# A differential attention and feed-forward block: projections and scores in split 16-bit halves, with scales worked out on chip

## The chip, the cores and the metric

The kernel runs on one core of one Trainium2 chip. The metric is the device time in microseconds of one execution. Engines are called PE (TensorE), DVE (VectorE), ACT (ScalarE), POOL (GpSimd) and SP (SyncE), as in the profile.

## The reference, cut to what matters

The input `x` is 2048 tokens of 256 numbers (float32). In short:

```python
def attn(x):
    qkv = x @ Wqkv.T + bqkv            # 16 query heads, 8 key heads of 128; 4 value heads of 256
    # 8 output heads; head h has two maps, each with its own query and key head
    p1 = softmax(causal(q[h, 0] @ k[h // 2, 0].T / sqrt(128)))
    p2 = softmax(causal(q[h, 1] @ k[h // 2, 1].T / sqrt(128)))
    o = (p1 - lam * p2) @ v[h // 2]    # lam from four vectors
    o = o / rms(o) * subln_w * (1 - LAMBDA_INIT)
    return concat(o) @ out_w.T + out_b

def ffn(x):                            # fwht: normalised Walsh-Hadamard transform
    x = fwht(x * SU_ug) / 64
    x = silu(x @ W_gate.T * s_gate) * (x @ W_up.T * s_up)
    return fwht(x * SU_dp) / 64 @ W_down.T * s_down

x = x + layernorm(attn(layernorm(x)))
x = x + layernorm(ffn(layernorm(x)))
```

All inputs and the output are float32.

## The kernel before, in words

**Split products.** A product of float32 matrices is made of three matmuls: each factor is split into a high half (a rounded copy, written by ACT) and a low half (what is left, written by DVE as source minus high half), and high x high, high x low and low x high are summed in PSUM. For the input, the weights of queries, keys and values, and the queries and keys themselves the halves are `float32r` (tiles `xT_hi`/`xT_lo`, `wq_*`, `wkv_*`, `q_*`, `k_*`). The probabilities, the values, the attention output and its weights are already split in 16-bit halves (`p16`, `v16`, `o16`, `wo16`), with a scale that keeps them in the range of the type: for the values `v_scale`, from a bound that is worked out on chip from the sum of squares of the weights (steps CV and CS).

**Tiling.** Tokens are cut in 16 tiles of 128. The 4 groups (one value head each, two key heads `m`, four query heads) are worked through in turn. A group has 16 duos (`d`, 64 in all), a duo two query tiles (`o`), a long and a short one, together 17 key blocks of 128, in 5 chunks `j` of up to 512 keys. For each duo and map `m` a step S makes the scores of a chunk: three matmuls (lines 1038, 1041, 1044) into one of four score banks. DVE then takes the chunk's maximum (line 1441), or, for the last chunk of a tile, adds the causal mask and takes the maximum in one instruction (line 1436; line 1431 where the tile has one chunk only, directly with the sign turned). If the tile has more chunks than one, line 1445 reduces the maxima to `negmx`, after a wait for the instruction before it. ACT's step E (line 1211) takes the exponential out of the score bank, with `negmx` as bias and the sum of the row as a second result. The query weights hold the factor 1/sqrt(128) already (`scale=SCALE` in WQ), so the exponential's scale is the constant 1.0 or -1.0. DVE then makes `ratio` and `gain` (SUMS, INV, GAIN: lines 1718, 1723, 1733, 1736). The second map's exponentials are scaled by `ratio` on ACT (line 1226) or POOL (line 1782), added to the first's on POOL (line 1749), split in halves on ACT (line 1233) and DVE (line 1452), transposed by DMA, and multiplied with the values in step PV (lines 1065 to 1067). The output of a tile is normed (lines 1241, 1708, 1756, 1249, 1482), transposed by DMA and multiplied with the output weights in step OP (line 1118).

**Projections.** QP makes a query head for 256 tokens (six matmuls, line 1137; halves by lines 1267 and 1494), K a key head for 512 tokens (line 1082; 1275 and 1502), V the values of 256 tokens (line 1100; 1515, 1280, 1790). They are six matmuls per 256 or 512 columns (V: twelve). The keys of the next group are written over those of this one, so that K of map 0 stands among the last scores of a group, and K of map 1 among the first of the next.

**Order of the work.** `plan()` goes through the whole work once, ahead of time, with a cost and a rank for each step of each engine (`add(...)` in `spawn`), and what it depends on (`needs`). PE takes the first step of its streams that may start; another engine takes the ready one of the lowest rank. The result is a fixed order of instructions for each engine; at run time each engine goes through its list in order and waits on semaphores. The start is written out by hand in `FIRST_STEPS`: LN and NX norm the input, X transposes it (line 1020; 1291 and 1547), IDLE are transposes of no use that keep PE busy, and WK, WQ, WV split the weights (ACT lines 1304, 1297, 1307; DVE lines 1567, 1557, 1571). CQ and CV (DVE lines 1462 and 1468, PE line 1050) and CS (DVE line 1476, POOL lines 1814 to 1822) work out the scale of the values. SP's queue loads at the start, in this order: two pieces of `x`, the key and value weights of the first group, a third piece of `x`, `col` (columns of biases and scales), the lambda vectors, `bv` (the value biases, broadcast), `out_b_row`. ACT's queue loads two pieces of `x`, the query weights of the first group and a last piece of `x`.

**The feed-forward part.** Its weights are folded with the transform on the chip in the last group: HAD and FB on POOL, FH (lines 1334, 1616), the matmul F (line 1147) and its eviction by ACT (line 1352) and DVE (line 1624) into places that `wug` names, among them the last quarter of `k_hi` and `k_lo` (F 0 and 1), `wq_hi` and `wq_lo` (F 4 and 5). F 0 and 1 therefore wait for the last score that reads a late key (`last_late_key`), F from 4 for the last query projection. Z transposes the normed rows into the columns of `xT_*` that queries no longer need (line 1154; 1367, 1640), and waits for a late query projection. Evictions of F and Z have rank 2. A step that holds one of the four work banks of PSUM (`turn_bank` 0 and 1, `sum_bank`, `proj_bank`) keeps it until its eviction has run, and PE's next step for that bank waits. G and U (line 1172) are the gate and up products, DN (lines 1189, 1191) the down product.

## Time and profile before

| | us |
|---|---|
| median of 3 runs | 1286.78 |
| lowest and highest | 1283.31, 1291.37 |
| the profiled execution | 1285.75 |
| its span in the trace | 1283.5 |

The span runs from the first to the last instruction of the profiled execution; some 2 us lie around it. A row of a group gives engine, line, operation, output<-inputs, shapes and count, then the busy time in us and the mean of one in ns, and after the second bar the idle time of the engine just before these instructions and what ended it. PEld are PE's weight loads, which overlap its matmuls. Matmuls overlap each other too, so their pace is read from start to start in a timeline, not from their length. A clock of 1.00 in a window is the full 2.4 GHz.

### The profile page before, as it was taken

To read this page: it belongs to the slowest core of one execution; us is meant where nothing else is said; L and a number is where in the kernel's file an instruction comes from. 1 tells how busy PE (TensorE), PEld (TensorE's weight loads), DVE (VectorE), ACT (ScalarE), POOL (GpSimd) and SP (SyncE) were. 2 spreads that over 40 slices of the span, in tenths; PEclk is the share of its full clock that TensorE was granted. 3 is DMA by queue.
4 is the path that set the end of the run, shared out by engine and by line. 5 is a ranking of instruction groups with operands and counts; after the bars stand their busy time and mean duration, and the time that the engine had idled before them with its cause. 6 is when DMAs were issued, how large, how long until landed. Compare 5 with 4: busy or idle time off the path is not lost.

```text
span 1283.5 us, 26516 instructions
## 1 busy us (share of the span) xinstructions
PE 1210.5 (94%) x8102; PEld 1018.7 (79%) x8102; DVE 1066.1 (83%) x2876; ACT 995.4 (78%) x2599; POOL 700.8 (55%) x797
## 2 busy tenths in 40 slices
PE   8899999999999999999999999999988797898998
PEld 7787887877888878888878788788876685786887
DVE  6889999888789998989799989888889899637545
ACT  5788888889688888978789889887877788745341
POOL 3464645454655655536565655445588574556532
PEclk9899999999999999999999999999998899999999
DMA  3145545564265554532555455445543453720001
GB/s 128 57 76 105 88 85 89 102 101 71 50 127 90 99 91 89 103 70 55 126 97 95 85 94 102 74 75 114 100 85 76 93 90 69 143 46 1 29 17 37
DMA packets 368154, 106.62 MB, mean 83 GB/s; under 512 B 359312, under 2 KB 365712, under 8 KB 367504
## 3 DMA queue, kind: packets, MB, share of 16 engines
q1 hardware_dynamic: 366672, 103.37, 42.6%
q8 instruction: 67, 1.10, 0.4%
q10 hardware_dynamic: 1344, 1.57, 0.3%
q14 instruction: 71, 0.58, 0.1%
HBM read 14.71 MB, written 2.10 MB: 13 GB/s over the span
## 4 chain that ended last, share of the span: by engine, by line
PE 47%; DVE 29%; issue 8%; ACT 8%; POOL 4%; DMA 4%; SPq 1%; ACTq 0%; DVEq 0%; POOLq 0%
DVE p L1452 7%; PE score_bank L1172 7%; DVE mx L1441 6%; PE score_bank L1038 5%; PE score_bank L1044 4%; PE score_bank L1041 4%; ACT e_all L1211 4%; DVE score_bank L1436 4%; PE turn_bank L1065 2%; POOL e_all L1749 2%; PE turn_bank L1066 2%; PE turn_bank L1067 2%; DMA p16T<-p 2%; PE proj_bank L1065 2%; PE proj_bank L1067 2%
## 5 line engine op out<-in xcount | busy, mean ns | idle before, releaser
L1749 POOL TENSOR_TENSOR e_all<-e_all 128x512 f32<-128x512 f32 (+3 forms) x320 | 372.9, 1179 | 141.9 <-ACT e_all L1226 131.6
L1211 ACT ACTIVATE e_all<-score_bank,negmx 128x512 f32<-128x512 f32 (+2 forms) x640 | 394.1, 625 | 60.8 <-DVE negmx L1445 46.3
L1038 PE MATMUL score_bank<-k_hi,q_hi 128*128 128x512 f32 (+2 forms) x640 | 257.1, 402 | 32.9 <-ACT e_all L1211 16.9
L1452 DVE SCALAR_TENSOR_TENSOR p<-e_all,gain,p 128x512 f16<-128x512 f32 (+3 forms) x320 | 266.2, 846 | 9.3 <-ACT p L1233 8.9
L1441 DVE TENSOR_REDUCE mx<-score_bank 128x1 f32<-128x512 f32 (+1 forms) x384 | 242.5, 636 | 18.3 <-PE score_bank L1044 17.4
L1041 PE MATMUL score_bank<-k_lo,q_hi 128*128 128x512 f32 (+2 forms) x640 | 233.0, 364 | 0.4 <-DVE k_lo L1502 0.4
L1044 PE MATMUL score_bank<-k_hi,q_lo 128*128 128x512 f32 (+2 forms) x640 | 233.1, 364 | 0.0
L1233 ACT ACTIVATE p<-e_all,gain 128x512 f16<-128x512 f32 (+3 forms) x320 | 203.9, 665 | 13.0 <-POOL e_all L1749 12.6
L1038 PEld LDWEIGHTS score_bank<-k_hi,q_hi 128*128 128x128 f32 x640 | 121.7, 190 | 75.6 <-ACT e_all L1211 33.6
L1782 POOL TENSOR_SCALAR e_all<-e_all,ratio 128x512 f32<-128x512 f32 (+3 forms) x123 | 89.6, 728 | 156.8 <-DVE ratio L1733 155.9
L1756 POOL TENSOR_TENSOR few<-few,half_neg 128x1 f32<-128x1 f32 x128 | 78.5, 614 | 142.0 <-DVE few L1708 141.8
L1065 PE MATMUL turn_bank<-v,p16T 128*128 128x256 f16 x553 | 152.4, 276 | 3.7 <-DVE q_lo L1494 1.7
L1066 PE MATMUL turn_bank<-v,p16T 128*128 128x256 f16 x553 | 151.6, 274 | 0.0
L1067 PE MATMUL turn_bank<-v,p16T 128*128 128x256 f16 x553 | 151.5, 274 | 0.0
L1226 ACT ACTIVATE e_all<-e_all,ratio 128x512 f32<-128x512 f32 (+2 forms) x197 | 121.5, 660 | 16.5 <-DVE ratio L1733 16.3
L1044 PEld LDWEIGHTS score_bank<-k_hi,q_lo 128*128 128x128 f32 x640 | 121.5, 190 | 14.0
L1211 ACT ACTIVATION_READ_ACCUMULATOR e_all<-score_bank,negmx 128x1 f32 x640 | 131.9, 206 | 0.0
L1041 PEld LDWEIGHTS score_bank<-k_lo,q_hi 128*128 128x128 f32 x640 | 122.3, 191 | 7.0 <-DVE k_lo L1502 0.6
L1436 DVE CUSTOM_DVE_ANT_0 score_bank<-score_bank,mask 128x384 f32<-128x384 f32 (+2 forms) x192 | 110.7, 577 | 14.7 <-PE score_bank L1044 14.3
L1065 PE MATMUL proj_bank<-v,p16T 128*128 128x256 f16 x326 | 89.4, 274 | 0.0
L1067 PE MATMUL proj_bank<-v,p16T 128*128 128x256 f16 x326 | 89.0, 273 | 0.0
L1066 PE MATMUL proj_bank<-v,p16T 128*128 128x256 f16 x326 | 89.0, 273 | 0.0
(393 smaller groups left out, 2738.6 us busy)
## 6 DMA issues: line engine op xcount, KB each, us to landing
p16T<-p SPq DMA_TRANSPOSE x320, 3.1
w_raw<-in_w_qkv_dram SPq DMA_DIRECT2D x3, 1024.0 KB, 5.3
w_raw<-in_w_o_dram SPq DMA_DIRECT2D x4, 512.0 KB, 3.3
oT<-o SPq DMA_TRANSPOSE x128, 2.5
bv<-in_hidden_dram SPq DMA_DIRECT2D x8, 256.0 KB, 2.9
w_raw<-in_w_ug_dram SPq DMA_DIRECT2D x4, 512.0 KB, 4.3
out_dram<-e SPq DMA_DIRECT2D x16, 128.0 KB, 1.7
e<-in_w_d_dram SPq DMA_DIRECT2D x1, 1024.0 KB, 5.9
```

Of the source, the lines that this page charges most:

```text
L1038: pe.matmul(bank[:, 0:w], qh, kh, start=True, stop=False)
L1041: pe.matmul(bank[:, 0:w], qh, kl, start=False, stop=False)
L1044: pe.matmul(bank[:, 0:w], ql, kh, start=False, stop=True).then_inc(s_full, 1)
L1065: pe.matmul(bank[:, 0:HID], hi, v16[:, kt, 0, :], start=(kt == 0), stop=False)
L1066: pe.matmul(bank[:, 0:HID], hi, v16[:, kt, 1, :], start=False, stop=False)
L1067: mm = pe.matmul(bank[:, 0:HID], lo, v16[:, kt, 0, :], start=False, stop=(kt == i))
L1211: act.activation(e, S[k % NS][:, 0:w], ACT.Exp, bias=negmx[:, d % 2, m, s:s + 1], scale=-1.0 if alone else 1.0, accum_out=ssum[:, d % 4, s ...
L1233: act.activation(halves_of(q, w)[0], e1_of(q, w), ACT.Copy, scale=gain[:, d % 4, s:s + 1]).then_inc(p_hi, 1)
L1436: dve.tensor_tensor_reduce(out=S[k % NS][:, 0:w], in0=S[k % NS][:, 0:w], in1=mask[:, BANK - w:], scale=1.0, scalar=LOWEST, op0=ALU.add, op ...
L1441: dve.tensor_reduce(mx[:, d % 2, m, s, c:c + 1], S[k % NS][:, 0:w], X, ALU.max)\
L1452: dve.scalar_tensor_tensor(out=halves_of(q, w)[1], in0=e1_of(q, w), scalar=gain[:, d % 4, s:s + 1], in1=halves_of(q, w)[0], op0=ALU.mult, ...
L1749: pool.tensor_tensor(a, a, b, ALU.add).then_inc(p_pool, 1)
```

## The change

The input (`x16`, scaled by 8), the weights (`wq16`, `wkv16`), the queries (`q16`) and the keys (`k16`) become 16-bit halves. The scales of queries, keys and values come from bounds worked out on chip: CQ squares the query weights on ACT, CV the biases and the key and value weights on DVE, PE adds over the partitions with two matmuls, CS on DVE and POOL makes `w_scale` and `scale` and scales the biases `col` and `bv`, and a new step CU on DVE makes `unit`, 1/sqrt(128) over the product of the scales of queries and keys. The scores are then `1/unit` too large in PSUM; the exponential takes `unit` as its scale, the maxima are multiplied with it. WK, WQ and WV of a group wait for CS. Keys lie in two buffers, used in turn by the groups. Homes of feed-forward weights and rows move to where no score or query of the last group reads, and the waits of F and Z for them go. In `plan()` some costs are changed, and evictions of F and Z get better ranks.

```diff
 FIRST_STEPS = (
-    ("LN", 0), ("LN", 1), ("NX", 0), ("WK", 0), ("NX", 1), ("IDLE", 38), ("X", 0), ("X", 1), ("IDLE", 8),
-    ("X", 2), ("X", 3), ("IDLE", 8), ("WQ", 0), ("LN", 2), ("K", (0, 1, 0)), ("K", (0, 0, 0)),
+    ("LN", 0), ("LN", 1), ("NX", 0), ("NX", 1), ("CQ", 0), ("IDLE", 38), ("X", 0), ("X", 1), ("CV", 0), ("CS", 0),
+    ("IDLE", 8), ("X", 2), ("X", 3), ("WK", 0), ("WQ", 0), ("LN", 2), ("IDLE", 8), ("K", (0, 1, 0)), ("K", (0, 0, 0)),
...
-SCORE_US, VALUE_US = 0.00136, 0.00257
+SCORE_US, VALUE_US = 0.00129, 0.00257
...
-            add("S", "DVE", "S", what, (0.17 if last else 0.07) + 0.00104 * w + (0.15 if last and c else 0), [pe], 0)
+            unit = [] if d % DUOS else [("DVE", "CU", d // DUOS)]
+            add("S", "DVE", "S", what, (0.17 if last else 0.07) + 0.00104 * w + (0.25 if last and c else 0), [pe] + unit, 0)
...
-                    "WK": [("PE", "V", (g - 1, V_UNITS - 1))] if g else [], "WV": [("POOL", "CS", g)]}[kind]
+                    "WK": [("PE", "V", (g - 1, V_UNITS - 1))] if g else [], "WV": []}[kind] + [("POOL", "CS", g)]
...
         elif kind == "CQ":
-            add("Y", "DVE", "CV", what, 1.1, [], 1)
+            add("Y", "ACT", "CQ", what, 1.1, [], 1)
+            add("Y", "DVE", "CV", what, 2.4, [], 1)
         elif kind == "CS":
             add("Y", "DVE", kind, what, 0.2, [("PE", "CV", what)], 0)
-            add("Y", "POOL", kind, what, 1.6, [("DVE", kind, what)], 0)
+            add("Y", "POOL", kind, what, 2.8, [("DVE", kind, what)], 0)
+            add("Y", "DVE", "CU", what, 0.6, [("POOL", kind, what)], 0)
...
         elif kind == "Z":
-            add("O", "ACT", kind, what, 0.7, [pe], 2)
-            add("O", "DVE", kind, what, 0.72, [("ACT", kind, what)], 2)
+            add("O", "ACT", kind, what, 0.7, [pe], 0)
+            add("O", "DVE", kind, what, 0.72, [("ACT", kind, what)], 1)
...
         elif kind == "F":
-            add("O", "ACT", kind, what, 0.7, [pe], 2)
-            add("O", "DVE", kind, what, 0.75, [("ACT", kind, what)], 2)
+            add("O", "ACT", kind, what, 0.7, [pe], 0)
+            add("O", "DVE", kind, what, 0.75, [("ACT", kind, what)], 1)
...
         if kind == "F":
-            return [("DVE", "FH", what)] + ([("PE", "S", last_late_key)] if what < 2 else
-                                             [("PE", "QP", (ALL_DUOS // 2 - 1, 1, 1))] if what >= 4 else [])
+            return [("DVE", "FH", what)]
         if kind == "Z":
-            return [("ACT", "N", (what[0], 3, half)) for half in range(2)] + [("PE", "QP", (ALL_DUOS // 2 - 5, 1, 1))]
+            return [("ACT", "N", (what[0], 3, half)) for half in range(2)]
...
-        xT_hi = sb("xT_hi", [P, CT, SEQ], F32R)
-        xT_lo = sb("xT_lo", [P, CT, SEQ], F32R)
+        zT_at = sb.at()
+        zT = sb("zT", [P, FFN_CHUNKS, 2, CT, BANK], F32R)
+        x16 = placer(nc, zT_at + 16 * CT * BANK)("x16", [P, 2, CT, SEQ], F16)
...
+            k16 = placer(nc, sa.at())("k16", [P, 2, 2, 2, SEQ], F16)
             k_hi = sa("k_hi", [P, 2, SEQ], F32R)
             k_lo = sa("k_lo", [P, 2, SEQ], F32R)
...
-                        kh = k_hi[:, m, key:key + w]
-                        kl = k_lo[:, m, key:key + w]
+                        kh = k16[:, d // DUOS % 2, m, 0, key:key + w]
+                        kl = k16[:, d // DUOS % 2, m, 1, key:key + w]
...
-                                   scale=-1.0 if alone else 1.0, accum_out=ssum[:, d % 4, s, m, c:c + 1]).then_inc(s_act, 1)
+                                   scale=-1.0 if alone else unit[:, g], accum_out=ssum[:, d % 4, s, m, c:c + 1]).then_inc(s_act, 1)
...
                             dve.tensor_tensor_reduce(out=S[k % NS][:, 0:w], in0=S[k % NS][:, 0:w],
-                                                     in1=mask[:, BANK - w:], scale=-1.0, scalar=HIGHEST,
+                                                     in1=mask[:, BANK - w:], scale=neg_unit[:, g], scalar=HIGHEST,
...
                             dve.wait_ge(s_dve, k + 1)
-                            dve.tensor_reduce(negmx[:, d % 2, m, s:s + 1], mx[:, d % 2, m, s, 0:c + 1], X,
-                                              ALU.max, negate=True).then_inc(neg_ready, 1)
+                            dve.tensor_reduce(neg_raw[:, d % 2, m, s:s + 1], mx[:, d % 2, m, s, 0:c + 1], X,
+                                              ALU.max, negate=True).then_inc(raw_ready, 1)
+                            dve.wait_ge(raw_ready, neg_use[o, m] + 1)
+                            dve.tensor_tensor(negmx[:, d % 2, m, s:s + 1], neg_raw[:, d % 2, m, s:s + 1], unit[:, g],
+                                              ALU.mult).then_inc(neg_ready, 1)
...
                     elif kind == "CV":
                         if what == 0:
+                            dve.wait_ge(cols_landed, 16)
+                            dve.wait_ge(rows_landed, 32)
+                        else:
+                            dve.wait_ge(bound_full, what)
+                        at = K_COL + 2 * what
+                        for n, bias in ((0, col[:, 4 * what:4 * what + 4]), (1, col[:, at:at + 2]), (2, bv[:, what, :])):
+                            dve.tensor_tensor_reduce(out=squares_b[:, n, 0:bias.shape[-1]], in0=bias, in1=bias,
+                                                     scale=1.0 / P if n == 2 else 1.0, scalar=0.0, op0=ALU.mult,
+                                                     op1=ALU.add, accum_out=wb_sq[:, n:n + 1]).then_inc(sq_ready, 1)
+                        if what == 0:
                             dve.wait_ge(first_w_landed, 16)
...
+                        for n in (1, 2):
+                            part = w_raw[:, :, BANK + (n - 1) * HID:BANK + n * HID]
+                            dve.tensor_tensor_reduce(out=squares_w[:, n - 1, :, :], in0=part, in1=part, scale=float(HID),
+                                                     scalar=0.0, op0=ALU.mult, op1=ALU.add,
+                                                     accum_out=w_sq[:, n:n + 1]).then_inc(sq_ready, 1)
...
+                    elif kind == "CU":
+                        g = slice(what, what + 1)
+                        dve.wait_ge(scale_ready, 2 * what + 2)
+                        dve.tensor_tensor(both[:, 0:1], scale[:, what, 0:1], scale[:, what, 1:2], ALU.mult)\
+                           .then_inc(unit_step, 1)
+                        dve.wait_ge(unit_step, 2 * what + 1)
+                        dve.reciprocal(both[:, 1:2], both[:, 0:1]).then_inc(unit_step, 1)
+                        dve.wait_ge(unit_step, 2 * what + 2)
+                        dve.tensor_scalar(unit[:, g], both[:, 1:2], SCALE, None, ALU.mult).then_inc(unit_ready, 1)
+                        dve.tensor_scalar(neg_unit[:, g], both[:, 1:2], -SCALE, None, ALU.mult).then_inc(unit_ready, 1)
```

The 16-bit forms of the other instructions follow the same pattern: `x16`, `wq16`, `wkv16`, `q16` in the place of the float32r tiles, in QP, K, V and X. ACT's WQ, WK and WV read their scale per partition from `w_scale`.

## Rows read from the trace of the kernel before

**Rows 1.** The page, part 1: busy time, share of the span, instructions of each engine.
```profile
PE 1210.5 (94%) x8102; PEld 1018.7 (79%) x8102; DVE 1066.1 (83%) x2876; ACT 995.4 (78%) x2599; POOL 700.8 (55%) x797
```

**Rows 2.** Busy time by windows: length, engines' busy us (instructions), clock, DMA share, GB/s.
```profile
100.00:900.00 800.00, 776.81 (x5485) 656.72 (x5484) 709.93 (x1935) 682.72 (x1834) 434.61 (x475) 1.00 0.50 91
400.00:500.00 100.00, 97.64 (x687) 81.55 (x685) 92.88 (x260) 90.90 (x250) 59.03 (x65) 1.00 0.50 88
600.00:700.00 100.00, 97.64 (x725) 83.76 (x725) 85.18 (x237) 80.58 (x218) 54.84 (x59) 1.00 0.52 100
900.00:1130.00 230.00, 199.86 (x1361) 164.70 (x1360) 195.66 (x524) 179.79 (x476) 146.06 (x173) 0.95 0.50 94
1130.00:1283.00 153.00, 145.03 (x718) 119.79 (x716) 82.01 (x190) 62.08 (x116) 73.93 (x82) 0.99 0.07 21
```

**Rows 3.** Timeline of PE from 400 us: start us, length us, engine, line, operands.
```profile
399.84 0.27 PE L1065 MATMUL turn_bank<-v,p16T 128*128 128x256 f16 x1
...
400.71 0.27 PE L1067 MATMUL turn_bank<-v,p16T 128*128 128x256 f16 x1
...
401.18 0.40 PE L1038 MATMUL score_bank<-k_hi,q_hi 128*128 128x512 f32 x1
...
401.88 0.40 PE L1137 MATMUL sum_bank<-xT_hi,wq_hi 128*128 128x256 f32 x2
...
402.58 0.39 PE L1038 MATMUL score_bank<-k_hi,q_hi 128*128 128x512 f32 x1
```

**Rows 4.** Groups by line: weight loads, float32 and 16-bit; busy us, mean ns, idle before.
```profile
L1041 PEld LDWEIGHTS score_bank<-k_lo,q_hi 128*128 128x128 f32 x640 | 122.3, 191 | 7.0 <-DVE k_lo L1502 0.6
...
L1066 PEld LDWEIGHTS turn_bank<-v,p16T 128*128 128x128 f16 x553 | 54.6, 99 | 5.7
```

**Rows 5.** Groups by line and form on ACT: busy us, mean ns, idle us before.
```profile
L1211 ACT ACTIVATE e_all<-score_bank,negmx 128x512 f32<-128x512 f32 x320 | 217.9, 687 | 45.3 <-DVE negmx L1445 37.9 <-DMA p16T<-p 5.7 <-DVE negmx L1431 0.2
...
L1375 ACT ACTIVATE acc<-acc,n_shift,n_rs 128x256 f32<-128x256 f32 x16 | 8.5, 591 | 0.3 <-POOL n_shift L1874 0.3
...
L1226 ACT ACTIVATE e_all<-e_all,ratio 128x256 f32<-128x256 f32 x7 | 3.5, 503 | 0.3 <-DVE ratio L1733 0.2
...
L1291 ACT ACTIVATE xT_hi<-turn_bank 128x512 fp32r<-128x512 f32 x4 | 2.3, 596 | 1.6 <-PE turn_bank L1020 1.6
...
L1352 ACT ACTIVATE spare<-turn_bank,su_s 128x512 fp32r<-128x512 f32 x2 | 1.4, 688 | 0.2 <-PE turn_bank L1147 0.2
```

**Rows 6.** Timeline of DVE from 441.98 us.
```profile
441.98 0.14 DVE L1436 DVE_READ_ACCUMULATOR2_ANT mx<- 128x1 f32 x1
442.15 0.16 DVE L1445 TENSOR_REDUCE negmx<-mx 128x1 f32<-128x3 f32 x1
442.23 0.22 DVE L1733 SCALAR_TENSOR_TENSOR ratio<-s,inv,neg_lam 128x1 f32<-128x1 f32 x1
```

**Rows 7.** Groups by line on DVE: negmx, and two low halves.
```profile
L1494 DVE SCALAR_TENSOR_TENSOR q_lo<-turn_bank,bq,q_hi 128x256 fp32r<-128x256 f32 x65 | 30.8, 475 | 2.4 <-ACT q_hi L1267 2.2
...
L1482 DVE SCALAR_TENSOR_TENSOR o<-turn_bank,few,o 128x256 f16<-128x256 f32 x63 | 30.0, 477 | 10.0 <-ACT o L1249 9.9
...
L1445 DVE TENSOR_REDUCE negmx<-mx 128x1 f32<-128x2 f32 (+1 forms) x192 | 29.9, 156 | 6.6
```

**Rows 8.** Timeline of the start, all engines.
```profile
4.13 0.68 SPq L914 DMA_DIRECT2D bv<-in_rows_dram  x1
...
15.24 0.71 PE L1082 MATMUL turn_bank<-xT_hi,wkv_hi 128*128 128x512 f32 x2
...
28.28 0.68 DVE L1462 CUSTOM_DVE_ANT_1 squares<-w_raw 128x512 f32<-128x512 f32 x1
...
31.39 0.19 POOL L1817 TENSOR_SCALAR few<-few 128x1 f32<-128x1 f32 x1
```

**Rows 9.** DMA issues: queue, operation, count, KB each, us to landing.
```profile
bv<-in_rows_dram SPq DMA_DIRECT2D x1, 512.0 KB, 9.9
```

**Rows 10.** Waits of PE, 1000 to 1060 us: us in total, times, longest us.
```profile
PE turn_bank L1137 <- DVE spare L1624: 6.9, 1, 6.9
```

More of the change, by code:

```diff
@@ L429, in needs @@
         if kind == "CV":
-            return [("DVE", "CV", what)]
+            return [("DVE", "CV", what), ("ACT", "CQ", what)]
         if kind == "OV":
@@ L1290, in _ @@
                         act.wait_ge(t_full, t_use[kind, what] + 1)
[L1291 to L1293 removed]
+                        act.activation(x16[:, 0, ct, q * BANK:(q + 1) * BANK], bank_for(kind, what)[:, :], ACT.Copy,
+                                       scale=X_UNIT).then_inc(t_hi, 1)
+                    elif kind == "CQ":
@@ L1294, in _ @@
                         act.wait_ge(w_landed, 16 * (2 * what + 1))
                         if what > 0:
+                            act.wait_ge(bound_full, what)
+                            act.wait_ge(sq_ready, 5 * what)
+                        act.activation(squares[:, :, :], w_raw[:, :, 0:BANK], ACT.Square, scale=float(HID) ** 0.5,
+                                       accum_out=w_sq[:, 0:1]).then_inc(sqq_ready, 1)
+                    elif kind == "WQ":
+                        act.wait_ge(scale_ready, 2 * what + 2)
+                        if what > 0:
```

297 lines of the change are left out of this document (144 added, 153 removed), and 4 rows, old and new, of the table FIRST_STEPS.

## The prediction

> **What bounds the kernel now.** I read the page first: the reader is to see PE busy for 94% of the span, DVE for 83%, ACT for 78%, POOL for 55% [rows 1]. Overlapping matmuls make a busy PE say little, so I took the windows next [rows 2]. In 100 to 900 us DVE is busy 709.9 and ACT 682.7 of 800 us. This stretch is no uniform one: of its eight windows of 100 us, four look like 400 to 500 us (DVE 92.88, ACT 90.90) and four like 600 to 700 us (DVE 85.18, ACT 80.58). After 900 us PE loses its density (199.9 of 230), and from 1130 us the feed-forward part runs, which the change leaves in float32.
>
> Third, the timeline of PE gives the pace from start to start [rows 3]. Eight 16-bit matmuls of 256 columns lie between 399.84 and 400.71: 0.1088 us each. Three float32 ones of 512 columns take 401.18 to 401.88, 0.2333 each, and six of 256 columns take 401.88 to 402.58, 0.1167 each. In 100 to 900 us the groups by form count 3021 matmuls of the first kind, and float32 columns worth 1803 matmuls of 512 columns: 1803 x 0.2333 + 3021 x 0.1088 = 749 us, 94% of the stretch. In 400 to 500 us the same sum gives 93.8, in 600 to 700 us 95.0. So PE bounds the light windows alone, while in the heavy ones DVE and ACT stand one to three points behind it. That is what decides this change: it takes work from PE and gives work to the two next in line.
>
> **What PE saves.** Scores, queries, keys and values turn 16-bit. No row has a 16-bit matmul of 512 columns; two of 256 make 0.2175, so I take 0.0158 saved per 512 columns. Bounds: zero, and 0.0316 if the fixed part of a matmul were all that changed. Scores: 3 x 278,528 columns are 1632 such units, 25.8 us; queries (128 x 6 of 256 columns) and values (32 x 12 of 256) 576 units, 9.1 us; keys (32 x 6) 192 units, 3.0 us. Sum 38 us, of which 1803 x 0.0158 = 28.5 fall in 100 to 900 us. Weight loads shrink from 191 to 99 ns [rows 4]; that is hidden while PE streams and is worth 0.09 us only where PE had waited, so I count it within the bounds.
>
> **What ACT gains.** The exponential (L1211) had a scale written into the instruction and a bias read per partition; now 576 of its 640 instructions (all but the 64 of rows of one chunk) read both per partition. Rows on what one such operand costs: Copy of 512 columns out of PSUM 596 ns with none, 688 ns with one; 256 columns in SBUF 503 ns with one, 591 ns with two [rows 5]. So 0.09 us each, 576 x 0.09 = 52 us, 40 of them in 100 to 900 us, 5.0 per window. Bounds: zero and 0.09. No row has an exponential with both.
>
> The Trainium skill (ScalarE: Activation LUTs, section "What ACT_TABLE_LOAD costs") says that each such pointer operand adds about 93 ns. The rows agree with 92 and 88 ns; for the exponential with two, no row here shows it, and by the page the term would be 54 us. It is the rule that speaks most against this change.
>
> CQ adds one square over 1024 columns per group on ACT; from 596 ns for 512 columns I estimate 1.0 to 1.3 us, four times, 5 us spread out. WK and WV keep their length but for one operand.
>
> **What DVE gains.** Each of the 192 masked maxima with more chunks than one now ends in two small instructions, the negated maximum and its product with `unit`, and the second waits for the first. The row for such a wait is the accumulator read at 441.98, followed by L1445 at 442.15: 0.17 us; with no dependence the next starts 0.08 us later, at 442.23 [rows 6]. I take 0.17 (the new one waits the same way): 192 [rows 7] x 0.17 = 33 us, 25 of them in 100 to 900 us, 3.1 per window. Bounds 0.08 and 0.25, so 15 to 48 us. Queued behind it stand the next maximum and the low halves; the exponential waits for it, and PE's next score for the bank.
>
> The Trainium skill (VectorE: DVE Perf Modes, section "The DRAIN you can't avoid") holds that a semaphore after every instruction costs nothing extra. The row here shows 0.09 us more with the wait than without, for instructions this small; by the page this term would be 15 us and the total some 5 us lower.
>
> The 64 single-chunk maxima (L1431) read their scale per partition: between 0 and 0.09 us by ACT's rows, 3 us. The low halves cost the same in either type: 475 ns to float32r, 477 ns to 16 bits [rows 7]; zero, hidden or not. CV grows by three sums of squares and CU adds four small instructions: about 1.6 us per group, 6 us. POOL's CS grows by some 1.2 us per group; POOL's 45% of idle covers it, except at the start.
>
> **The main stretch.** A heavy window after: PE 93.8 - 3.4 = 90.4, DVE 92.9 + 3.1 = 96.0, ACT 90.9 + 5.0 = 95.9. Before, DVE had 7.1 and ACT 9.1 us of idle there. With all of it kept the window takes 103 to 105, with half kept 99.5 to 100.5; I take 101.5, since in-order engines that wait for each other keep some. A light one: PE 95.0 - 3.4 = 91.6, DVE 88.3, ACT 85.6: PE still ends last, with its former 5 us of gaps 96.6; I take 97. Four of each: 794, so 6 us are won of 800. Ends: all of PE's 28.5 won; 20 lost (105 four times).
>
> **The start.** All projections now wait for the scales. DVE's CV begins with the biases, and `bv` is issued at 4.13 and lands 9.9 later, at 14.0 [rows 8, 9]; nothing behind CV on DVE (the low halves of X) runs before. Before, the same chain from squares (28.28) to the scale on POOL (31.39 + 0.19) took 3.3 us [rows 8]; with four more sums, some 1.5 us, it ends near 18.8. ACT's WK (0.75) brings the first key to 19.6, where it started at 15.24 [rows 8]. 4.3 later, less a little since CV, CS no longer break in at 28 us: +4. Ends 0 and +8, the upper one if PE's clock falls in the pause. The cover is gone here: nothing else can run.
>
> **The last group.** Keys of group 3 lie in the second buffer, and z in columns of its own, so F and Z need no late score or query any more, and their evictions get the first rank on ACT. That removes the wait of a query projection for the bank that an F held, 6.9 us [rows 10], and perhaps 5 us of smaller ones and of lowered clock (0.95 in 900 to 1130 us [rows 2]). DVE is late next: its 195.7 us of 230 grow by 7. Net -5; ends -20 and +7. The two key buffers move no key projection: the list of steps keeps their places. They are costed at nothing, for PE's order already kept them apart. The feed-forward part: 0, within 2.
>
> **Sum.** Against the profiled execution (1285.75 us for a span of 1283.5): 1285.75 + 4 - 6 - 5 = 1278.75, say 1279. That execution lies 1.0 under the median of the runs shown (1286.78), well inside their spread, so I add nothing.
>
> **Rivals.**
> *PE stays the only bound.* For it: PE's sum is the highest in every window, and the gaps of DVE are mostly waits for others. Against it: DVE and ACT at 96% of a heavy window. Then 38 us go, and of the last group 7: 1285.75 + 4 - 38 - 7 = 1245; half way to it is likelier, so 1250.
> *ACT takes PE's place.* The exponential's second operand, in heavy windows: ACT keeps the 9.1 us it waits for maxima and lands at 105, while `plan` still gives E its old cost and moves no scaling to POOL. It decides once ACT stays above some 91% busy, its share there now. 4 x 5 = 20, start 4, the last group nothing: 1310. Against it: PE's and DVE's earlier scores shorten those waits.
> *The last group clears wholly* (-20, the rest as forecast): 1264.
> *The 16-bit matmuls stream no faster at 512 columns,* so the change doesn't do what it says: the heavy windows slow, the light ones stay, 1296.
>
> **How the numbers follow.** Chances: the forecast 0.42 (its own range 1266 to 1292), PE alone 0.25, ACT 0.22, the last group 0.07, no faster stream 0.04. Range 1252 to 1304: it cuts the outer half of the two large rivals. About 1% (1274 and 1300) is what a measurement of this kernel can tell from no change. Faster by over 1%: 0.25 + 0.07 + 0.07 of the forecast's own 0.42 = 0.39. Slower: 0.19 of ACT's 0.22 and 0.01 of the last = 0.20. Between: 0.41.
>
> **What would show it.** L1211's successor at about 0.09 us more for each form; negated maximum and product 0.17 us apart, 192 times; score matmuls of 512 columns near 0.2175 us; the first key near 19.6 us; in heavy windows DVE and ACT at 95% or more and PE's sum near 90; no wait of PE for a held F bank. Wrong it would be if the exponential kept 687 ns, if heavy windows held no more than 93% of DVE (then PE alone bounds), or if the first key came by 16 us.

## The result and the profile after

| | us |
|---|---|
| before, median of 4 runs | 1285.43 |
| after, median of 4 runs (1333.32 to 1337.74) | 1334.20 |
| ratio, 95% interval | 1.0377 [1.0336, 1.0417] |
| after, the profiled execution and its span | 1334.5, 1332.7 |
| forecast (range) | 1279 (1252 to 1304) |

The change costs 49 us where the forecast had it win 7. The page of the kernel after, part 1 (busy time by engine) and the first line of part 4 (the chain that ended last, by engine):

```profile
PE 1184.8 (89%) x8110; PEld 831.2 (62%) x8110; DVE 1133.7 (85%) x3107; ACT 1040.1 (78%) x2596; POOL 700.3 (53%) x820
...
DVE 48%; PE 21%; issue 11%; ACT 10%; DMA 6%; POOL 2%; SPq 1%; ACTq 0%; DVEq 0%; POOLq 0%
```

Against [rows 1], PE lost 26 us of busy time and five points of its share. DVE gained 68 us, ACT 45. Nearly half of the chain now runs over DVE, where the page of before has 47% of it on PE and 29% on DVE:

```profile
PE 47%; DVE 29%; issue 8%; ACT 8%; POOL 4%; DMA 4%; SPq 1%; ACTq 0%; DVEq 0%; POOLq 0%
```
The windows, columns as in [rows 2]:

```profile
100.00:900.00 800.00, 722.42 (x5185) 493.62 (x5186) 722.98 (x2006) 681.73 (x1749) 414.87 (x472) 0.99 0.48 85
400.00:500.00 100.00, 88.48 (x631) 59.57 (x628) 94.53 (x280) 86.32 (x222) 55.92 (x64) 0.98 0.50 88
600.00:700.00 100.00, 91.67 (x701) 66.33 (x700) 89.70 (x255) 81.32 (x211) 55.97 (x58) 1.00 0.48 89
900.00:1130.00 230.00, 199.02 (x1442) 137.85 (x1439) 211.84 (x568) 191.18 (x481) 143.37 (x173) 0.99 0.48 89
```

In 800 us PE gets through 5185 matmuls where it got through 5485, though each is cheaper. DVE is busier in every window, ACT not: ACT's share fell in 400 to 500 us from 90.9 to 86.3, so it waits. For whom, the waits say (us in total, times, longest):

```profile
ACT e_all L1225 <- DVE negmx L1465: 83.2, 113, 2.5
...
PE score_bank L1050 <- ACT e_all L1225: 41.3, 68, 2.3
...
PE score_bank L1050 <- issue: 28.5, 50, 2.2
```

The exponential waits 83 us for the scaled maximum; before, it waited 46 for the maximum. Groups by line and form on ACT and DVE:

```profile
L1225 ACT ACTIVATE e_all<-score_bank,negmx,few 128x512 f32<-128x512 f32 x304 | 234.4, 776 | 79.0 <-DVE negmx L1465 72.1 <-DMA p16T<-p 5.3 <-DVE p L1472 1.1
L1225 ACT ACTIVATE e_all<-score_bank,negmx,few 128x384 f32<-128x384 f32 x256 | 170.8, 672 | 15.9 <-DVE negmx L1465 11.1 <-DMA p16T<-p 4.4
...
L1465 DVE TENSOR_TENSOR negmx<-few 128x1 f32<-128x1 f32 x192 | 74.0, 385 | 6.6
```

The first answers to the 687 ns of [rows 5]: 776, the 0.09 us of the forecast. The last is the surprise: a product of one number per partition, at 385 ns on average, 74 us in all. Its line by itself (shortest, median and longest in ns) shows that most are short and some very long:

```profile
L1465 DVE TENSOR_TENSOR negmx<-few x192: 159/161/1282, 33.2 to 1162.4; 128x1 f32<-128x1 f32 x192
```

Two timelines of the same moment, DVE's and then POOL's, show what a long one is:

```profile
1124.64 0.16 DVE L1462 TENSOR_REDUCE few<-mx 128x1 f32<-128x3 f32 x1
1124.83 1.26 DVE L1465 TENSOR_TENSOR negmx<-few 128x1 f32<-128x1 f32 x1
1126.01 0.68 DVE L1458 TENSOR_REDUCE mx<-score_bank 128x1 f32<-128x512 f32 x1
```

```profile
1124.02 0.70 POOL L1804 TENSOR_SCALAR e_all<-e_all,ratio 128x512 f32<-128x512 f32 x1
1124.81 1.26 POOL L1771 TENSOR_TENSOR e_all<-e_all 128x512 f32<-128x512 f32 x1
1126.06 0.59 POOL L1804 TENSOR_SCALAR e_all<-e_all,ratio 128x384 f32<-128x384 f32 x1
```

POOL's sum of the two maps starts at 1124.81 and ends at 1126.07; DVE's product starts 0.02 us behind it and ends at 1126.09. Over the whole trace, of the 81 products that start while POOL is idle none takes more than 0.25 us, of the 111 that start while POOL is at work 82 do. The reduce before it (L1462), with one tensor as input, takes 154 to 160 ns whatever POOL does.

Not every instruction of POOL holds the product up. Nine products start inside one of POOL's small powers (x to the -0.5, on one to four columns: L1778, L1904) with 0.16 us or more of it left, and all take 159 to 161 ns. This power runs from 140.61 to 141.16, and the product in it is short:

```profile
140.61 0.55 POOL L1778 TENSOR_TENSOR few<-few,half_neg 128x1 f32<-128x1 f32 x1
```

```profile
140.72 0.16 DVE L1465 TENSOR_TENSOR negmx<-few 128x1 f32<-128x1 f32 x1
```

The start, in the timeline (DVE's squares of the biases, PE's first matmul of the bounds, of a key and of a score):

```profile
15.07 0.16 DVE L1483 CUSTOM_DVE_ANT_0 squares_b<-col 128x4 f32<-128x4 f32 x1 [4.24 <-DMA out_b_row<-in_rows_dram]
```

```profile
17.04 0.59 PE L1063 MATMUL proj_bank<-few,ones 128*128 128x3 f32 x2 [6.63 <-DVE few L1492]
...
22.91 0.59 PE L1095 MATMUL turn_bank<-x,wkv 128*128 128x512 f16 x2
...
29.23 0.38 PE L1050 MATMUL score_bank<-k,q 128*128 128x512 f16 x1
```

The first key comes 7.7 us later than in [rows 8]. At the other end stand PE's last score matmuls, of before and of after:

```profile
1110.38 0.33 PE L1044 MATMUL score_bank<-k_hi,q_lo 128*128 128x384 f32 x1
```

```profile
1161.10 0.33 PE L1056 MATMUL score_bank<-k,q 128*128 128x384 f16 x1
```

They lie 51 us apart, so the whole loss stands ahead of the feed-forward part. Each of the four groups has 160 chunks of scores. Cut at every 160th of the chunks' last matmuls, the four stretches take 277.3, 282.3, 282.3 and 289.5 us, before 268.5, 264.8, 265.7 and 289.5: 8 us are lost before the first score, 43 in the first three stretches and none in the last.

### The profile page after: what moved, and what is told of

Its sections match the earlier page's. It is cut to its first block, busy times and chain, and to the rows that moved or that the text cites. A ratio compares the mean times of both kernels' runs of the same rounds, so it can differ in the third digit from the quotient of the medians.

```text
span 1332.7 us, 26815 instructions
## 1 busy us (share of the span) xinstructions
PE 1184.8 (89%) x8110; PEld 831.2 (62%) x8110; DVE 1133.7 (85%) x3107; ACT 1040.1 (78%) x2596; POOL 700.3 (53%) x820
## 4 chain that ended last, share of the span: by engine, by line
DVE 48%; PE 21%; issue 11%; ACT 10%; DMA 6%; POOL 2%; SPq 1%; ACTq 0%; DVEq 0%; POOLq 0%
DVE p L1472 11%; DVE mx L1458 9%; ACT e_all L1225 6%; PE score_bank L1185 6%; DVE score_bank L1453 6%; DMA p16T<-p 4%; DVE negmx L1465 3%; DVE q L1526 2%; DVE acc L1565 2%; DVE o L1514 2%; DVE few L1462 2%; PE score_bank L1050 1%; DMA oT<-o 1%; DVE ratio L1755 1%; PE score_bank L1056 1%
## 5 line engine op out<-in xcount | busy, mean ns | idle before, releaser
L1225 ACT ACTIVATE e_all<-score_bank,negmx,few 128x512 f32<-128x512 f32 (+2 forms) x576 | 413.3, 724 | 95.0 <-DVE negmx L1465 83.2
L1771 POOL TENSOR_TENSOR e_all<-e_all 128x512 f32<-128x512 f32 (+3 forms) x320 | 364.7, 1153 | 94.7 <-ACT e_all L1240 83.5
L1050 PE MATMUL score_bank<-k,q 128*128 128x512 f16 (+2 forms) x640 | 227.0, 355 | 74.6 <-ACT e_all L1225 41.3
L1472 DVE SCALAR_TENSOR_TENSOR p<-e_all,gain,p 128x512 f16<-128x512 f32 (+3 forms) x320 | 257.4, 822 | 5.2 <-ACT p L1247 4.9
L1053 PE MATMUL score_bank<-k,q 128*128 128x512 f16 (+2 forms) x640 | 225.9, 353 | 0.3 <-DVE k L1533 0.3
L1056 PE MATMUL score_bank<-k,q 128*128 128x512 f16 (+2 forms) x640 | 225.8, 353 | 0.0
L1804 POOL TENSOR_SCALAR e_all<-e_all,ratio 128x512 f32<-128x512 f32 (+2 forms) x134 | 92.8, 693 | 214.8 <-DVE ratio L1755 214.2
L1050 PEld LDWEIGHTS score_bank<-k,q 128*128 128x128 f16 x640 | 62.9, 98 | 176.0 <-ACT e_all L1225 82.1
L1778 POOL TENSOR_TENSOR few<-few,half_neg 128x1 f32<-128x1 f32 x128 | 78.8, 617 | 170.4 <-DVE few L1730 170.4
L1240 ACT ACTIVATE e_all<-e_all,ratio 128x384 f32<-128x384 f32 (+2 forms) x186 | 115.0, 659 | 8.9 <-DVE ratio L1755 8.2
L1225 ACT ACTIVATION_READ_ACCUMULATOR e_all<-score_bank,negmx,few 128x1 f32 x576 | 116.7, 203 | 0.0
L1056 PEld LDWEIGHTS score_bank<-k,q 128*128 128x128 f16 x640 | 63.3, 99 | 58.1 <-issue 3.5
L1078 PE MATMUL sum_bank<-v,p16T 128*128 128x256 f16 x306 | 84.6, 276 | 12.3 <-DMA p16T<-p 8.7
L1080 PE MATMUL sum_bank<-v,p16T 128*128 128x256 f16 x306 | 84.8, 277 | 0.0
L1079 PE MATMUL sum_bank<-v,p16T 128*128 128x256 f16 x306 | 84.6, 277 | 0.0
L1465 DVE TENSOR_TENSOR negmx<-few 128x1 f32<-128x1 f32 x192 | 74.0, 385 | 6.6
```

The costliest lines, as they stand in the source:

```text
L1050: pe.matmul(bank[:, 0:w], qh, kh, start=True, stop=False)
L1053: pe.matmul(bank[:, 0:w], qh, kl, start=False, stop=False)
L1056: pe.matmul(bank[:, 0:w], ql, kh, start=False, stop=True).then_inc(s_full, 1)
L1078: pe.matmul(bank[:, 0:HID], hi, v16[:, kt, 0, :], start=(kt == 0), stop=False)
L1079: pe.matmul(bank[:, 0:HID], hi, v16[:, kt, 1, :], start=False, stop=False)
L1080: mm = pe.matmul(bank[:, 0:HID], lo, v16[:, kt, 0, :], start=False, stop=(kt == i))
```

## The experiments

Three theories. **A:** DVE has become the bound, and the product is dear because its instruction, with two tensors in SBUF as inputs, is held up while POOL works. **B:** ScalarE's scale pointer costs it. **C:** the order that `plan` writes out. Ratios are to the kernel before, run on the same chip. Its median there was 1283.5 to 1286.5 us, so a difference of 2 or 3 us between kernels of different batches says nothing.

### The product, one edit at a time on the kernel after

**e1_ts** exchanges the instruction:

```diff
-dve.tensor_tensor(negmx[...], neg_raw[...], unit[:, g], ALU.mult)
+dve.tensor_scalar(negmx[...], neg_raw[...], unit[:, g], None, ALU.mult)
```

> The kernel after, with one instruction exchanged: the product that scales the row maximum (192 times a 128x1 result) reads its second factor as a per-partition pointer (tensor_scalar) and no longer as a second tensor (tensor_tensor). Theory A (VectorE has become the bound, and the product is dear because an instruction with two tensors in SBUF is held up while GpSimd works: mean 385 ns, shortest 159, longest 1282): the product falls to about 160 to 200 ns, VectorE gives back 35 to 43 us of busy time, and the time falls by at least 20 us, to 1295 to 1314. Theory B (ScalarE's second pointer on the exponential, 0.09 us each, some 52 us, is what costs): the product may get shorter, the time stays within 1% of 1334. Theory C (the new order of the engines' queues costs): the same, within 1%.

1305.2 us, ratio 1.0158 [1.0117, 1.0200]: 29 us back for one operand read another way, within theory A's range. Its line:

```profile
L1465 DVE TENSOR_SCALAR negmx<-few x192: 211/214/216, 33.2 to 1134.2; 128x1 f32<-128x1 f32 x192
```

It is slower than the shortest tensor_tensor (159) and never slower than 216. Two of A's figures are just missed: the product was to fall to 200 ns or less, and DVE was to give back at least 35 us; it gives back 33.6 (1100.1 for 1133.7). The exponential's wait for it falls from 83.2 to 53.8.

**e2_nomul** takes the product out, and leaves out the subtraction of the row maximum (the exponential still waits for the reduce):

```diff
-dve.tensor_reduce(neg_raw[...], mx[..., 0:c + 1], X, ALU.max, negate=True).then_inc(raw_ready, 1)
-dve.wait_ge(raw_ready, neg_use[o, m] + 1)
-dve.tensor_tensor(negmx[...], neg_raw[...], unit[:, g], ALU.mult).then_inc(neg_ready, 1)
+dve.tensor_reduce(negmx[...], mx[..., 0:c + 1], X, ALU.max, negate=True).then_inc(neg_ready, 1)
-act.activation(e, S[...], ACT.Exp, bias=negmx[...], ...)
+act.activation(e, S[...], ACT.Exp, bias=few[:, 116:117], ...)   # zeros
```

> The kernel after without the product: the row maximum is written by the reduce alone, and the exponential reads a column of zeros as its bias, so the subtraction of the row maximum is left out; its wait on the reduce stays, as does the scale pointer. Theory A: 74 us of VectorE's busy time go; the time falls by 40 us or more, to 1270 to 1295. Theory B: ScalarE is unchanged and the time stays at 1320 or above. Theory C: 1320 or above.

1282.2 us, 0.9976 [0.9957, 0.9994]. The product costs 52 us in all: 29 the stall, 23 the steady form of the instruction and its wait. DVE's busy time falls by 63.0 us (1070.7 for 1133.7), not by the 74 expected. A group's busy time adds up its instructions one by one, and the page counts the time in which they overlap once. Besides, DVE's low halves of the probabilities (`p`, also with two tensors in SBUF) take 262.5 us here for 257.4, which fits a part of the stall moving to another instruction.

**e3_imm** has an immediate for the scale pointer, and leaves out the right scale of the scores:

```diff
-scale=-1.0 if alone else unit[:, g], accum_out=...
+scale=-1.0 if alone else 1e-6, accum_out=...
```

> The kernel after with an immediate (1e-6) as the exponential's scale in place of the pointer (the right scale of the scores is left out); the product stays. ScalarE gives back about 0.09 us on 560 exponentials, 50 us. Theory B: the time falls by 30 us or more, to 1305 or lower. Theory A: the score bank comes free 0.09 us sooner at best, VectorE stays the bound: 1320 to 1334.

1318.5 us, 1.0267 [1.0227, 1.0306]: 16 us back, and one exponential of 512 columns takes 687 ns again. It falls between the theories: 1.5 us under what A allowed, 13 above what B wanted. ACT's busy time fell by 48 us, so a third of it shows.

**e4_both** has both edits of e2_nomul and e3_imm, and leaves out the same.

> Neither the product nor the pointer: bias a column of zeros, scale an immediate (row maximum and scale of the scores are left out). What is left of the change is 16-bit operands, the two key buffers, the bounds at the start and the order. If A or B or both hold, the time falls to 1245 to 1270, which is what the 40 us that TensorE saved allow with TensorE as the only bound. Theory C (order): it stays above 1285.

1268.5 us, 0.9877 [0.9839, 0.9915]: 14 us under e2_nomul. A and B add up: 52 and 14 to 16.

### The same two costs on the kernel before

**b_tt** and **b_ts** add the product to the kernel before, by a column of ones, in either form; **b_ptr** adds the pointer (`scale=-1.0 if alone else few[:, 54:55]`).

```diff
+dve.wait_ge(raw_ready, neg_use[o, m] + 1)
+dve.tensor_tensor(negmx[...], neg_raw[...], few[:, 54:55], ALU.mult)        # b_tt
+dve.tensor_scalar(negmx[...], neg_raw[...], few[:, 54:55], None, ALU.mult)  # b_ts
```

> The kernel before with the product alone: the row maximum is multiplied by a column of ones in a tensor_tensor of two SBUF operands, 192 times. Theory A (the instruction is held by GpSimd, whatever the rest): its mean is 300 to 450 ns with instances above 1 us, VectorE gets 60 to 85 us more, and the time rises by 15 to 50 us to 1300 to 1335. If only the kernel after's order makes the product dear, its mean is under 200 ns and the time stays within 1%.

> The kernel before with the product (by one) as a tensor_scalar, that is b_tt with its second factor read as a pointer. b_tt took 1331 us with a mean of 393 ns for the product. If the stall beside GpSimd is what costs, the product takes 211 to 216 ns always, and of b_tt's 46 us 25 to 32 come back: 1300 to 1308. If it is the additional instruction and its semaphore wait alone, the time stays at 1320 or above.

> The kernel before with the scale pointer alone (a column of ones) on the exponentials that had an immediate. ScalarE gets 0.09 us on 576 of them, 52 us. In the kernel after, the pointer was worth 16 us (1334 to 1318), without the product 14 us (1282 to 1268). If these add up with the rest: 1296 to 1302 here. If TensorE at 0.94 of its pace hides it: within 1% (up to 1297). If ScalarE becomes the bound: 1305 or more.

The product's group in b_tt, then in b_ts, then the exponential's in b_ptr:

```profile
L1453 DVE TENSOR_TENSOR negmx<-few 128x1 f32<-128x1 f32 x192 | 75.4, 393 | 6.7
```

```profile
L1453 DVE TENSOR_SCALAR negmx<-few 128x1 f32<-128x1 f32 x192 | 41.1, 214 | 6.9
```

```profile
L1211 ACT ACTIVATE e_all<-score_bank,negmx,few 128x512 f32<-128x512 f32 x304 | 234.7, 778 | 40.8 <-DVE negmx L1446 33.9 <-DMA p16T<-p 6.3
```

b_tt took 1331.1 us, 1.0366 [1.0346, 1.0387]; b_ts 1308.9, 1.0176 [1.0135, 1.0218]; b_ptr 1304.0, 1.0138 [1.0102, 1.0174]. So 192 products of 128 numbers turn the kernel before into one as slow as the kernel after, with PE in float32 and nothing else touched. The split of the product's busy time in DVE's page is as in e2_nomul: b_tt adds 52.3 us to it (the product's group 75.4), b_ts 27.6 (41.1). b_ts lies 1 us above what was expected. b_ptr lies between its cases: 45 us of ACT's busy time cost 17 to 20. PE's load hides neither.

### Other ways to the same number

**e_fused** multiplies and reduces in one instruction: `dve.tensor_scalar(mx[..., 0:c + 1], mx[..., 0:c + 1], neg_unit[:, g], HIGHEST, ALU.mult, ALU.min, accum_out=negmx[...])`.

> The kernel after with the reduce over the chunk maxima and the product drawn into one instruction: tensor_scalar multiplies the 2 to 4 maxima by the negated unit (a pointer) and keeps their minimum (accum_out). One VectorE instruction and one semaphore wait less per row tile than in e1_ts, but a read of the accumulator more (140 ns in the rows of such instructions). Theory A: VectorE's chain from the last score to the exponential is 156 + 385 ns in after, 156 + 214 in e1_ts and 156 in e2_nomul (1282 us); here some 200 + 140, near e1_ts: 1290 to 1305. Slower than e1_ts would speak against the count of instructions as the price.

1287.9 us, 1.0021 [1.0007, 1.0035], 2 us under its range. **g2** is e_fused with the ratio through pointers and a mended start:

```diff
-("X", 0), ("X", 1), ("CV", 0), ("CS", 0), ("IDLE", 8), ("X", 2), ("X", 3), ("WK", 0), ...
+("X", 0), ("X", 1), ("IDLE", 8), ("X", 2), ("X", 3), ("CV", 0), ("CS", 0), ("IDLE", 24), ("WK", 0), ...
...
-dve.scalar_tensor_tensor(out=ratio[...], in0=s12[...], scalar=inv[...], in1=neg_lam[:, 0:1], ...)
+dve.tensor_scalar(ratio[...], s12[...], inv[...], neg_lam[:, 0:1], ALU.mult, ALU.mult)
```

> e_fused, with the ratio too read with pointers (tensor_scalar for scalar_tensor_tensor, so that no small VectorE instruction reads two tensors in SBUF; 128 of them, mean 249 ns, up to 1173) and the start mended: VectorE squares the weights before the biases, the rows of the value bias are loaded ahead of the input's third part, and TensorE transposes input tiles 2 and 3 before the matmuls of the bounds. Theory A: 0 to 6 us from the ratio; the start gives 3 to 6 us (first key matmul at 17 to 19 us for 22.9): in all 4 to 12 us under e_fused. If the late start is hidden behind the later work, the landmarks move and the time does not.

1280.1 us, 0.9960 [0.9946, 0.9975]. The lines of the new instructions in g2:

```profile
L1462 DVE TENSOR_SCALAR_CACHE_REDUCE mx<-mx,few x192: 214/216/219, 27.6 to 1105.6; 128x2 f32<-128x2 f32 x64, 128x3 f32<-128x3 f32 x64, 128x4 f32<-128x4 f32 x64
L1462 DVE DVE_READ_ACCUMULATOR mx<-mx,few x192: 80/83/85, 27.7 to 1105.7; 128x1 f32 x192
```

```profile
L1753 DVE TENSOR_SCALAR ratio<-s,inv,neg_lam x128: 256/267/275, 46.1 to 1109.4; 128x1 f32<-128x1 f32 x128
```

The ratio gained nothing: 267 ns always, where e_fused had 264 on average (203 to 1170). With two pointers the steady form costs as much as the stalls. So g2's 8 us under e_fused are put down to the start, which also has DVE square the weights before the biases and `bv` loaded ahead of the input's third part. **e_start** has those edits alone, on the kernel after:

> The kernel after with the mended start alone (weights squared before biases, value bias rows loaded earlier, transposes of tiles 2 and 3 ahead of the bounds' matmuls). In g2 these edits moved the first score from 29.2 to 23.8 us. If the late start reaches the end undiminished, 1327 to 1330; if VectorE's load swallows it, 1333 or more.

1323.8 us, 1.0296 [1.0242, 1.0349]: 10 us. The first score moved by 5.8 (29.23 to 23.44). The late start reaches the end undiminished; that it costs more than those 5.8 is not shown, since the intervals of e_start and after touch.

What the start of after also had is a lower clock. PE's matmuls ended at 10.41 us, it waited until 17.04, and from about 12.5 to 22.7 us the granted clock was 0.50, that is 1.2 GHz, where the same stretch of e_start has the full clock. From 13 to 22 us, in after and then in e_start (the third number from the end):

```profile
13.00:22.00 9.00, 4.96 (x23) 4.96 (x24) 3.89 (x14) 1.09 (x4) 2.20 (x6) 0.50 0.12 46
```

```profile
13.00:22.00 9.00, 7.28 (x52) 5.03 (x50) 7.30 (x22) 4.52 (x9) 5.14 (x10) 1.00 0.14 46
```

Eight idle transposes took 1.95 us at the lower clock (from 17.91) and take 1.04 at the full one in e_start (from 10.27).

### The order

**e_cost** changes two numbers of the planner:

```diff
-add("S", "DVE", "S", what, ... + (0.25 if last and c else 0), ...)
+add("S", "DVE", "S", what, ... + (0.55 if last and c else 0), ...)
-add("E", "ACT", "E", (d, m, jj), 0.23 + 0.00084 * ww, ...)
+add("E", "ACT", "E", (d, m, jj), 0.34 + 0.00084 * ww, ...)
```

> The kernel after with the planner's costs as the trace has them: 0.34 us and not 0.23 fixed for the exponential, 0.55 and not 0.25 for the reduce over maxima with its product. Theory C (the order laid out for cheaper instructions costs time): the time falls by 10 us or more, to 1324 or lower. Theories A and B: within 6 us of 1334, since the engines' work is the same.

1315.7 us, 1.0233 [1.0180, 1.0285]: 18 us, which A and B had not left room for. DVE stays at 1130.5 us busy; the exponential waits 48.3 us for the product, for 83.2. `plan` also picks the engine that scales the second map's exponentials, ACT or POOL. Here that hardly changes: ACT scales 188 chunks (186 in after), POOL 132 (134). Each number was then changed alone, and both in the kernel before, where they are wrong:

> The kernel after with the planner's cost of the exponential alone raised (0.34 for 0.23 us fixed). e_cost, with both costs raised, took 1315.7 us, 18 less than after. In the trace of after one exponential of 512 columns holds ScalarE 0.76 us (start to start), where the planner has 0.66: this error came with the scale pointer. If this cost's error is what the order suffers from, 1314 to 1322; if the product's is, 1330 or more.

> The kernel after with the planner's cost of the reduce over maxima with its product alone raised (0.55 for 0.25 us). If the order suffers from the stalled product being unknown to the planner, 1314 to 1322; if from the exponential's cost, 1330 or more. If both give a part, 1322 to 1330 each. If any change of the costs scatters the time by some 10 us either way, neither this sum nor that of e_cost_e will fit 18.

> The kernel before with both planner costs raised as in e_cost (0.34 for 0.23, 0.45 for 0.15), although its instructions are as they were: its planner's costs are then too high by 0.1 and 0.3 us. If what helped in e_cost is that the costs were made right, the time stays or rises here (1283 to 1300). If dearer ScalarE and VectorE steps in the plan are better in themselves (more slack ahead of the scores), it falls to 1280 or lower.

e_cost_e: 1327.2 us, 1.0328 [1.0297, 1.0359]. e_cost_s: 1338.3, 1.0414 [1.0382, 1.0446]. b_cost: 1298.3, 1.0103 [1.0073, 1.0132]. Alone the two give -7 and +4, together -18; costs that are too high cost the kernel before 14. The intervals of e_cost_e and e_cost_s overlap that of after, and neither is the order alone: ACT scales 170 chunks in the first and 207 in the second, POOL the rest of the 320. e_cost and b_cost moved two chunks and one, so they do show what the order is worth: -18 and +14. So C is real but no clean term, and what the two costs do is not shown to add. **g3**, g2 with the exponential's cost at 0.34:

> g2 (1280 us: the scaling of the maximum in one instruction, the mended start) with the planner's exponential at 0.34 us. If the order was laid out wrong for the pointer, a part of the 18 us comes back here too: 1266 to 1276. If the order only mattered while VectorE was the bound: 1278 to 1283.

1277.6 us, 0.9952 [0.9931, 0.9972], no clear gain over g2, 2 us above the bracket for "a part comes back". As in e_cost_e, 16 scalings moved from ACT to POOL.

### What the 16-bit operands are worth

**f_fixed** keeps the 16-bit halves and both key buffers, and gives queries and keys fixed units, so that the score in PSUM is the logit. Their bounds, `unit`, the product and the pointer are gone, and the start is that of the kernel before. It is meant for inputs of about this size only; that far larger or smaller ones would overflow the halves or lose their digits was not tested. The ratio is read through pointers, as in g2:

```diff
-X_UNIT = 8.0
+X_UNIT = 0.0625; B_FIX = SCALE ** 0.5; W_FIX = B_FIX / X_UNIT
-act.activation(wq16[:, 0, :, :], w_raw[:, :, 0:BANK], ACT.Copy, scale=w_scale[:, 0:1])
+act.activation(wq16[:, 0, :, :], w_raw[:, :, 0:BANK], ACT.Copy, scale=W_FIX)
...
-scale=-1.0 if alone else unit[:, g], accum_out=...
+scale=-1.0 if alone else 1.0, accum_out=...
```

> The 16-bit halves and two key buffers kept, but queries and keys with fixed units (input by 1/16, weights of queries and keys so that a score comes out of the matmul as the logit), so that neither the product, nor the scale pointer, nor the bounds of queries and keys (squares, their matmuls and powers) are there; only the bound of the values stays, as in the kernel before. Such halves keep their digits only for inputs of about this size. The start is the kernel before's. Ratio with pointers as in g2. Theories A and B together: e4_both (1268 us) less the start's 5 to 8 us and the bounds: 1250 to 1265, TensorE the bound again as in the forecast's rival. If it stays at 1270 or above, something else of the change (the order, the last group) holds it.

1253.9 us, 0.9764 [0.9740, 0.9788], the fastest of all: 31 us under the kernel before, 80 under the kernel after. Its page, part 1, and two windows:

```profile
PE 1162.5 (93%) x8110; PEld 834.2 (67%) x8110; DVE 1055.3 (84%) x2875; ACT 986.3 (79%) x2596; POOL 698.3 (56%) x805
```

```profile
100.00:900.00 800.00, 756.11 (x5562) 532.74 (x5561) 712.69 (x1945) 683.40 (x1849) 434.56 (x484) 0.99 0.52 91
400.00:500.00 100.00, 96.53 (x729) 69.53 (x728) 92.53 (x263) 90.65 (x248) 53.30 (x60) 1.00 0.54 92
```

DVE and ACT stand in 400 to 500 us where they stood in [rows 2], and PE does 729 matmuls there for 687. The gain is not even, though. Cut at every 160th chunk of scores, the four stretches take 257.5, 263.0, 263.7 and 279.2 us, before 268.5, 264.8, 265.7 and 289.5. The first and the last win 11 and 10 us, the stretch behind the last score 8, and the two in the middle only 2 each. **f_cost** raises the planner's costs there as b_cost does, to ask whether that is one lucky order:

> f_fixed (1253.9 us) with the planner's costs raised as in b_cost, too high by 0.1 and 0.3 us; its instructions are as in f_fixed. b_cost rose by 14 us over before with the same edit. If the order matters as much here, where TensorE has 3% less to do: 1260 to 1270. If f_fixed's time was the luck of one order: the same or less, 1245 to 1254.

1263.0 us, 0.9821 [0.9789, 0.9853]: wrong costs take 9 of the 31 us, and 22 stay. Here too 13 scalings moved from ACT to POOL.

## Why the prediction was wrong

**What failed, first: the product's price.** The forecast took 0.17 us for each product, from the distance between two dependent small instructions [rows 6], with 0.25 as its upper bound: 33 us, at most 48. Measured is 385 ns on average, 74 us in its group and 63 in DVE's busy time (e2_nomul), and 52 us of the kernel's. The steady form is what the forecast had priced: 29.4 us of DVE's busy time (e1_ts against e2_nomul). The step asked only how long a small instruction is, not what its operands need. [rows 6] even held the answer's shape: the ratio (L1733) at 442.23, also with two tensors in SBUF, stands there with 0.22 us; its group in the trace of before has a mean of 294 ns and a longest of 1204. One row of 128 was taken for all of them, and the row of the group was not asked for.

The Trainium skill (SBUF — State Buffer, section "SBUF: two separate sides") says that a VectorE instruction with two SBUF inputs and a GpSimd instruction that reads SBUF exclude each other, the one that starts first holding the port for its whole length. The traces agree for POOL's sum of the maps: it starts first, and the product ends at 1126.09, the sum at 1126.07. They do not agree for POOL's powers, which read SBUF too and hold up none of the nine products inside them. The rule was not weighed in the forecast.

**Second: how much of an engine's added work shows.** The forecast let half of DVE's and ACT's idle time in heavy windows stay, and none of the light windows lengthen. With the product at the forecast's size (29 us on DVE for 33), e1_ts still took 1305 us. On the kernel before, 28 us more of DVE's busy time cost 22 us (b_ts) and 45 of ACT's cost 18 (b_ptr). By the pages' busy times, ACT moves the time by 0.3 to 0.4 us for each us added or taken away (b_ptr; e3_imm 16 for 48), DVE by 0.8 to 0.9 (b_ts; b_tt 46 for 52; e2_nomul against e1_ts 23 for 29; e1_ts 29 for 34). Outside this stands e_fused, which also changes the chain of waits: 17 for 17 against e1_ts, 6 for 12 against e2_nomul. DVE and ACT idle because they wait for each other through four score banks, and the maximum, its product and the exponential stand in one row on that ring. ACT was not the bound it had been in the rival "ACT takes PE's place": its share fell. The place was DVE's, and that rival was not written down. The loss came where the forecast had 6 us won: 43 us in the first three groups.

**Third, the start.** Forecast +4 with +8 as its end; the first key came 7.7 us late. The scale itself was ready at 19.5 us, for 18.8 forecast: DVE waited not for `bv` alone but for `out_b_row` behind it (15.07 for the 14.0 taken). The forecast did name what would make it +8, a fall of PE's clock in the pause, and that came: 0.50 from about 12.5 to 22.7 us. The rest was missed: CV stands ahead of X 2 and 3 in PE's order and held PE for 6.6 us, so ACT's copies of X 2 and 3 ran at 20.75 and 21.60, and WK behind them at 22.10. The time paid 10 us for it (e_start), or 8 (g2 against e_fused).

**Fourth, the order.** It was taken as given. The planner's exponential had kept its old cost, which the forecast saw and used only for a rival; with this cost and that of the maximum raised 18 us came back (e_cost). How much of the 49 us the new order cost by itself stays open.

**What was right.** The exponential at +0.09 us for each form (776 for 687). The pace of the 16-bit matmuls, with the rows of after:

```profile
451.40 0.38 PE L1050 MATMUL score_bank<-k,q 128*128 128x512 f16 x1
451.61 0.38 PE L1053 MATMUL score_bank<-k,q 128*128 128x512 f16 x1
451.83 0.38 PE L1056 MATMUL score_bank<-k,q 128*128 128x512 f16 x1
```

451.40 to 451.83 is 0.215 each, for the 0.2175 expected and 0.2333 in float32. Summed over all matmuls by form, PE's pace time falls from 1155 to 1115 us; the forecast said 38. The rival "PE stays the only bound", 1250, comes near what f_fixed measures, 1253.9, once product, pointer, bounds and start are away. That is partly luck: PE has only 36% of f_fixed's chain and DVE 35%, and the two middle groups gained 4 us between them, where the forecast had some 9 of PE's 38 us in each group. The low halves cost the same in both types (474 ns for the queries' in after). The 6.9 us wait for the F bank [rows 10] is gone, but nothing came of it in the kernel after: the last stretch of scores takes 289.5 us as before, with DVE busy 96.7 of 100 us in 1000 to 1100. The forecast had 5 us won there; f_fixed has 10.

**The sum with measured terms:** f_fixed 1254, start 10, pointer 14 to 16, product 52: 1330 to 1332, for 1334 measured. The terms come from different kernels and orders, each of which may stand off by what the order is worth, so this closeness is partly luck. The bounds of the later groups stand in no term. What of f_fixed's distance to before is PE's pace and what the lighter last group was not separated.

## What to carry to other kernels

An operand form is part of an instruction's price: beside GpSimd's large sums, a small VectorE instruction with two SBUF tensors lasts until the sum ends, while the same arithmetic on one number per partition with a pointer was steady; look at the shortest and the longest of a group and not at one row. Work added to an engine at 78 to 85% on a ring of few banks cost a third of its length (ACT) to nearly all of it (DVE) here, whatever engine the page calls the bound; sum an edit that spares one engine and loads two others with that share. Where the order is written out by a planner, its costs are part of the kernel: change them with the instructions, and run two orders before a gain of 1% is believed.

## What the hardware showed

- DVE tensor_tensor 128x1 with both inputs in SBUF: 159 ns when POOL is idle, up to 1282 beside a POOL tensor_tensor of 512 columns, ending with it; beside POOL's powers of one to four columns 159 to 161. tensor_scalar with one pointer 211 to 216, with two 256 to 275, in all of 192 and 128 instances.
- tensor_scalar with a reduction (`accum_out`) over 2 to 4 columns: 216 ns and an 83 ns read of the accumulator, which beats a 156 ns reduce and a 214 ns product behind a wait (1287.9 us for 1305.2).
- Nearly the same instructions in another order, chosen by costs 0.1 and 0.3 us apart, took 18 us less in 1334 (e_cost) and 14 more in 1284 (b_cost).
- PE waited from 10.41 to 17.04 us, and the granted clock stood at 0.50 from about 12.5 to 22.7; it was back at 1.00 after PE had been busy from 17.04 on.
